# Moving 88 additions of an expert sum from VectorE to GpSimd in a one-core vision tower kernel

## The reference

```
h = _L0_tok_ref(x, ...)                                 # spectral layers, then an MLP
h = _layernorm(h + _L0_attn_ref(h, Wq, bq, Wk, bk, Wv, bv))
h = _layernorm(h + _L0_ffn_ref(h, gate_w, gate_b, w1, b1, w2, b2))   # 8 experts, top 1, with a capacity
h = _layernorm(h + _L1_attn_ref(h, W0, b0, W1, b1))                  # two layers of a gated recurrence
h = _layernorm(h + _L1_ffn_ref(h, ..., gamma, beta))                 # 16 experts, top 2, own norm inside
```

## Time and profile before

| what | value |
|---|---|
| time, median of 3 runs | 2967.37 us (2964.72 to 2968.38) |
| profiled execution, time | 2959.79 us |
| its span in the trace | 2958.0 us |
| PE busy over the span | 2663.2 us (90%) |
| DVE busy | 2114.4 us (71%) |
| ACT busy | 1995.4 us (67%) |
| POOL busy | 69.5 us (2%) |
| token part (2540 us to the end): PE, DVE, POOL busy of 418 us | 360.66, 342.26, 20.76 us |

### The profile page before, as it was taken

How to read it: one execution, slowest core, us unless ns; L and a number is a source line. 1 busy time by engine, 2 the same in 40 slices (tenths; PEclk the granted TensorE clock), 3 DMA queues, 4 the chain that set the end, 5 groups by cost and what they waited for, 6 DMA issues and landing times.

```text
span 2958.0 us, 75928 instructions
## 1 busy us (share of the span) xinstructions
PE 2663.2 (90%) x28642; PEld 1565.3 (53%) x28642; DVE 2114.4 (71%) x4202; ACT 1995.4 (67%) x2415; POOL 69.5 (2%) x93
## 2 busy tenths in 40 slices
PE   5777789999898999898999977999999999899985
PEld 3444456666566666666666654444444444454432
DVE  6999776888776888766888854454544544488887
ACT  5888675677565777655777755787787878555652
POOL 0000000000000000000000002000000000100000
PEclk9999999999999999999999999999999999999997
DMA  3422264754355754455755542411111110012232
GB/s 98 134 104 110 76 206 156 246 182 171 134 189 168 223 186 175 163 165 161 219 194 183 182 152 55 100 61 51 47 50 51 61 51 14 26 35 89 71 93 57
DMA packets 122800, 361.57 MB, mean 122 GB/s; under 512 B 45878, under 2 KB 73814, under 8 KB 86806
## 3 DMA queue, kind: packets, MB, share of 16 engines
q1 hardware_dynamic: 99542, 185.95, 20.1%
q10 hardware_dynamic: 18432, 134.23, 11.2%
q0 software_dynamic: 4672, 39.20, 6.1%
HBM read 204.77 MB, written 154.53 MB: 121 GB/s over the span
## 4 chain that ended last, share of the span: by engine, by line
PE 74%; DVE 11%; issue 7%; ACT 6%; DMA 2%; ACTq 0%; SPq 0%; DVEq 0%; POOL 0%; POOLq 0%
PE pA L1540 16%; PE pA L1548 8%; PE pT L1635 8%; PE pS L1577 7%; PE pD L1624 5%; PE pD L1591 4%; PE pT L1566 4%; PE pD L1511 3%; PE pD L1606 3%; PE pA L1566 2%; DVE arena L1907 2%; PE pT L1645 2%; ACT h_rows L1724 2%; DMA h_scratch<-h_new 1%; PE pS L1465 1%
## 5 line engine op out<-in xcount | busy, mean ns | idle before, releaser
L1874 DVE TENSOR_REDUCE small<-arena 128x32 f32<-128x1056 f32 x320 | 397.1, 1243 | 310.1 <-ACT arena L1709 303.5
L1540 PEld LDWEIGHTS pA<-conv_bd,h_in 128*128 128x128 f32 x4096 | 481.5, 193 | 95.3 <-issue 95.3
L1540 PE MATMUL pA<-conv_bd,h_in 128*128 128x128 f32 x4096 | 518.3, 280 | 2.1 <-DVE arena L1867 1.7
L1699 ACT COPY w_sb<-pA 128x1024 f32<-128x1024 f32 x256 | 259.4, 1013 | 249.9 <-PE pA L1548 232.5
L1720 ACT ACTIVATE h_new<-pT,bet,gam 128x1024 f32<-128x1024 f32 x256 | 307.1, 1200 | 148.9 <-PE pT L1566 132.4
L1888 DVE SCALAR_TENSOR_TENSOR w_sb<-w_sb,small 128x1024 f32<-128x1024 f32 x320 | 386.8, 1209 | 4.5 <-DVE h_new L1896 2.3
L1709 ACT ACTIVATE arena<-w_sb 128x1024 f32<-128x1024 f32 x320 | 338.9, 1059 | 10.2
L1577 PEld LDWEIGHTS pS<-cst,h_new 128*128 128x128 f32 x2048 | 220.4, 141 | 203.1 <-issue 133.3
L1566 PE MATMUL pT<-cst,w_sb 128*128 128x128 f32 x2048 | 276.1, 279 | 39.1 <-DVE w_sb L1888 20.2
L1577 PE MATMUL pS<-cst,h_new 128*128 128x128 f32 x2048 | 280.3, 280 | 23.3 <-ACT h_new L1720 20.8
L1566 PEld LDWEIGHTS pT<-cst,w_sb 128*128 128x128 f32 x2048 | 231.0, 143 | 104.1 <-DVE w_sb L1888 49.1
(11 more groups left out here) (325 smaller groups left out, 3427.9 us busy)
## 6 DMA issues: line engine op xcount, KB each, us to landing
h_scratch<-h_new ACTq DMA_DIRECT2D x128, 1024.0 KB, 4.4
h_in<-h_scratch SPq DMA_DIRECT2D x128, 1024.0 KB, 5.0
w_sb<-gates_scratch SPq DMA_DIRECT2D x168, 128.0 KB, 3.0
y_scratch<-w_sb POOLq DMA_DIRECT2D x32, 576.0 KB, 8.5
y_in<-y_scratch SPq DMA_DIRECT2D x512, 36.0 KB
w_sb<-in_L_tok_w1r_dram POOLq DMA_DIRECT2D x8, 576.0 KB, 7.0
w_sb<-in_L_tok_w1i_dram POOLq DMA_DIRECT2D x8, 576.0 KB, 6.7
w_sb<-in_L_tok_w2r_dram POOLq DMA_DIRECT2D x8, 576.0 KB, 6.9
```

What stands on the lines that cost most here:

```text
L1540: pe.matmul(pA[:, c:c + 128], h_in[:, 1024 * n + c:1024 * n + c + 128], conv_bd[:], start=(j == 0), stop=False, skip_group_check=True)
L1699: act.copy(raw[n], pA[:]).then_inc(s["copied"], 1)
L1874: dve.reduce_sum(var[n], sq[n % 2], axis=AX).then_inc(s["summed"], 1)
```

## The change

DVE no longer makes the additions of the expert sum. It multiplies each expert's bank with the gates into one of four buffers (two more than before, z3c and z3d, placed behind the other parameters), and POOL adds the buffer to Y. ADDS numbers the additions; a new semaphore `added` counts them. DVE waits before a product until the addition that read its buffer four before is done, and before the bias until all additions so far are done. POOL waits for its own previous addition and until DVE has freed the bank of this step. The gate stores stay in POOL's queue, now between additions. TOKEN_ORDER is a new list with the same steps in another order.

```
-        b2a, b2b, ge2 = param(P, S), param(P, S), param(P, 512)
+        b2a, b2b, ge2, z3c, z3d = param(P, S), param(P, S), param(P, 512), param(P, 512), param(P, 512)
...
-        Z3 = [w_sb[:, 2 * CW + CW * i:3 * CW + CW * i] for i in range(2)]
+        Z3 = [w_sb[:, 2 * CW + CW * i:3 * CW + CW * i] for i in range(2)] + [z3c, z3d]
...
+            if key[0] in ("out1", "out2"):
+                ADDS.append(ADDS[-1] + (key[2] > 0) if ADDS else -1)
...
                     if e == 0:
                         dve.tensor_tensor(y, b[:], GB[i % NGB], ALU.mult).then_inc(s["td_free"], 1)
-                        own_freed()
                     else:
-                        dve.tensor_tensor(Z3[e % 2], b[:], GB[i % NGB], ALU.mult).then_inc(s["td_free"], 1)
-                        own_freed()
-                        dve.tensor_tensor(y, y, Z3[e % 2], ALU.add)
+                        if ADDS[i] >= len(Z3):
+                            dve.wait_ge(s["added"], ADDS[i] - len(Z3) + 1)
+                        dve.tensor_tensor(Z3[ADDS[i] % len(Z3)], b[:], GB[i % NGB], ALU.mult).then_inc(s["td_free"], 1)
...
             def add_bias(c):
                 b = take()
-                link(dve.memset(score[:, 0:1], 0.0))
+                dve.wait_ge(s["added"], ADDS[used[0] - 1] + 1)
...
+                elif key[0] in ("out1", "out2"):
+                    i = uses
+                    uses += 1
+                    if key[2] > 0:
+                        if ADDS[i] > 0:
+                            pool.wait_ge(s["added"], ADDS[i])
+                        pool.wait_ge(s["td_free"], n_d + 4)
+                        pool.tensor_tensor(chunk(Y, c), chunk(Y, c), Z3[ADDS[i] % len(Z3)], ALU.add).then_inc(s["added"], 1)
```

Of the list, the last line before and now:

```
-    e2.2 e2.2 e2.3 e2.3 e2.3 eb2.2 e2.3 e2.3 e2.3 e2.3 yb2.2 e2.3 e2.3 e2.3 e2.3 e2.3 e2.3 e2.3 e2.3 e2.3 eb2.3 yb2.3
+    e2.2 eb2.2 e2.3 e2.3 yb2.1 e2.3 e2.3 e2.3 e2.3 e2.3 yb2.2 e2.3 e2.3 e2.3 e2.3 e2.3 e2.3 e2.3 e2.3 e2.3 eb2.3 yb2.3
```

More of the change, by code:

```diff
@@ L179 @@
 TOKEN_ORDER = """
[L180 to L187, removed]
-    e2.2 e2.2 e2.3 e2.3 e2.3 eb2.2 e2.3 e2.3 e2.3 e2.3 yb2.2 e2.3 e2.3 e2.3 e2.3 e2.3 e2.3 e2.3 e2.3 e2.3 eb2.3 yb2.3
+    xt1.0 qkv.0 xt1.1 sc.0 ex.0 qkv.1 pt.0 pv.0 xt1.2 qkv.2 xt1.3 wg.0 xt2.0 sc.1 gq1.0 gl1.0 ex.1 sc.2 pt.1 gx1.0 ex.2 cum.0 pv.1
+    qkv.3 gt1.0 pt.2 e1.0 xt2.1 e1.0 pv.2 gq1.1 e1.0 e1.0 sc.3 ex.3 gl1.1 gx1.1 e1.0 cum.1 pt.3 e1.0 pv.3 xt2.2 e1.0 e1.0 gt1.1
+    eb1.0 e1.1 e1.1 yb1.0 e1.1 e1.1 xt3.0 gq1.2 gru0.0 gl1.2 e1.1 gru1.0 e1.1 gback.0 gx1.2 e1.1 cum.2 xt4.0 xt2.3 gq2.0 gt1.2
+    gl2.0 gq1.3 gx2.0 gm2.0 e1.1 eb1.1 gt2.0 e2.0 e2.0 e2.0 e2.0 e2.0 e2.0 yb1.1 e2.0 e2.0 gl1.3 e2.0 gx1.3 xt3.1 e2.0 e2.0 e2.0
+    gru0.1 e2.0 e2.0 e2.0 e2.0 gru1.1 cum.3 e1.2 e1.2 gback.1 e1.2 e1.2 eb2.0 xt4.1 yb2.0 e1.2 e1.2 gt1.3 e1.2 e1.2 eb1.2 e1.3
+    e1.3 gq2.1 yb1.2 e1.3 gl2.1 e1.3 xt3.2 e1.3 gru0.2 e1.3 gru1.2 gx2.1 e1.3 gm2.1 gback.2 e1.3 eb1.3 gt2.1 e2.1 e2.1 e2.1 e2.1
+    e2.1 e2.1 yb1.3 xt4.2 e2.1 e2.1 xt3.3 e2.1 gru0.3 gq2.2 e2.1 e2.1 gru1.3 gl2.2 e2.1 e2.1 gx2.2 gm2.2 e2.1 e2.1 gback.3 e2.1
+    gt2.2 e2.2 e2.2 e2.2 e2.2 e2.2 e2.2 xt4.3 e2.2 e2.2 gq2.3 e2.2 e2.2 e2.2 gl2.3 gx2.3 gm2.3 e2.2 eb2.1 e2.2 gt2.3 e2.2 e2.2
+    e2.2 eb2.2 e2.3 e2.3 yb2.1 e2.3 e2.3 e2.3 e2.3 e2.3 yb2.2 e2.3 e2.3 e2.3 e2.3 e2.3 e2.3 e2.3 e2.3 e2.3 eb2.3 yb2.3
 """
@@ L424, in build @@
         g2_dram = nc.dram_tensor("gates2_scratch", [NCH, E2, CT * P], F32, kind="Internal").ap()
-        GT_PLACE, EB_FREED, sends_d = {}, {}, 0
+        GT_PLACE, EB_FREED, ADDS, sends_d = {}, {}, [], 0
         for key in token_steps():
@@ L442, in build @@
                   "scored", "gru_act", "gru_out", "ones_set", "passed",
-                  "attended", "fed", "recurred", "pair_subbed", "pair_exped", "pair_gated", "mixed1", "mixed2",
+                  "attended", "fed", "recurred", "pair_subbed", "pair_exped", "pair_gated", "mixed1", "mixed2", "added",
                   "gates_stored", "ge10_loaded", "ge11_loaded", "ge20_loaded", "ge21_loaded"] + [f"g_loaded{i}" for i in range(NGB)]
@@ L1031, in token_pool @@
                 pool.tensor_tensor(lo.bitcast(F32R), w, hi, ALU.subtract).then_inc(s["w1_split"], 1)
-            n_s = 0
+            n_s, n_d, uses = 0, 0, 0
             for key in token_steps():
+                n_d += TOKEN_SENDS.get(key[0], (0, 0))[0]
                 n_s += TOKEN_SENDS.get(key[0], (0, 0))[1]
```

## The result

The changed kernel took 2980.62 us, the median of 10 runs (2969.03 to 2987.24); the kernel before took 2967.84 us beside it, also 10 runs (2953.95 to 2971.68). The ratio is 1.0051 with a 95% interval of [1.0033, 1.0069]: slower by half a per cent.

What follows compares the result with a forecast made beforehand. PE was taken to bound the middle, three DVE normalisations the end. End steps gave 2954.4, less 5 for the middle: 2949.4 of span, 8.6 less than before; off the median, 2958.8 us, 8-in-10 range 2949 to 2973.

Steps and rivals of the forecast that it cites:

- The middle: Token part before 2865 us: fewer PE waits against new DVE and GpSimd waits, 5 us gained; bounds 13 gained, 5 lost.
- Goes: VectorE loses 0.72 us per expert, 63 us in all, mostly where PE bounds, which buys nothing by itself.
- Comes: Each 128x512 addition on GpSimd takes 1.27 us, one following another at 1.36 us.
- The shared path: Products run freely beside GpSimd's additions; two-SBUF instructions of a normalisation wait for them, 1.7 us in the sum.
- rival (d): Products and additions exclude each other, each addition costing 2.0 us instead of 1.36: 2992 us, chance 0.05.
- rival (c): Stores and additions delay each other in GpSimd's queue; bias waits 44 us, locks 18 us: 2975.8 us, chance 0.14.
- The end, steps 2 to 6: From `yb2.1` through `yb2.2` and nine experts to the last bias, then 25.55 us unchanged: span end at 2954.4.
- Step 1: PE finishes sending expert 1 of chunk 3 at 2881.8 instead of 2893.67, as stops and slow clock go.

Runs made afterwards that it cites:

- e1: The changed kernel with gate stores issued by ScalarE behind its copy, GpSimd having only additions: 2956.98 us, ratio 0.998 to the kernel before.
- e5: The kernel before, additions still on VectorE, with only the gate stores moved from GpSimd to ScalarE: 2966.41 us, ratio 1.000 to the kernel before.
- e11: The changed kernel measured and profiled again without an edit: 2975.67 us, ratio 1.0042 to the kernel before.
- e2: The changed kernel with the old list of steps, gate stores still on GpSimd: 2971.2 us, ratio 1.0027 to the kernel before.
- e4: The changed kernel with the old list of steps and gate stores issued by ScalarE: 2962.3 us, ratio 0.9992 to the kernel before.

## Why the prediction was wrong

The step that failed is the one named "The middle": "I take 5 us gained", with a loss of 5 as its bound, "if two new stops of 2.5 us appear". Three appeared, of 2.25, 2.88 and 6.24 us, each with slow matmuls behind it. TensorE's waits in the middle came to 18.2 us, where they were 10.2, and its clock to 0.96 where it was 0.99, another 9 us by the prediction's own measure (0.03 of 290 us). So the 5 us gained were some 13 us lost. `yb2.1` started 354.7 us behind the cast (2895.76 - 2541.05) where the steps put it at 336.9 (2877.6 - 2540.71): 18 us late. Without GpSimd's place and wait (e1) it started at 2881.91 - 2544.84 = 337.1 us. That agreement with the forecast is partly luck: the sum started from one profile with a token part of 417.3 us, and e5, timed the same, had 407.7. Timed, e1 gains 0.2%, about 6 us, where 8.6 were forecast.

The working had the parts. It said that GpSimd stands still at each store and that the loads behind it take 3.0 us. But it priced the store's landing, and never asked what stands *ahead* of the store in GpSimd's queue. The answer was in the new list: `gback.3 e2.1 gt2.2` and `gback.2 e1.3 eb1.3 gt2.1` put one product behind a normalisation on VectorE, its addition ahead of the store on GpSimd. The step also took "TensorE bounds this stage" as cover for VectorE's waits; a wait for gates isn't covered by VectorE's idle time, because TensorE runs out of banks.

Point by point:
- **Goes.** Right: VectorE's busy time over the span fell from 2114.4 to 2065.9 us, by 48.5; 60.9 us of additions went, and 8.3 of the other 12.4 us are in instructions that became longer beside GpSimd's (below). In the middle it bought nothing by itself, as said.
- **Comes.** Right: additions took 1.28 us (1.27 forecast), one behind another at 1.35 (1.36):

```profile
L1051 POOL TENSOR_TENSOR h_new<-h_new,spec 128x512 f32<-128x512 f32 x44 | 56.4, 1283 | 109.5 <-DVE spec L914 105.1 <-DVE w_sb L914 1.4 <-DMA gates_scratch<-h_in 1.3
```

- **The shared path.** Right, and with it rival (d) is out: products beside additions took 0.69 us. The second early instruction of `yb2.2` waited for the addition that had started before it, and ended 0.55 us behind it (2915.62 + 1.62 = 2917.24 against 2916.12 + 1.67 = 2917.79):

```profile
2914.72 1.37 DVE L809 SCALAR_TENSOR_TENSOR h_new<-w_sb,h_new 128x512 f32<-128x512 f32 x1
2916.12 1.67 DVE L810 TENSOR_TENSOR w_sb<-h_new 128x512 f32<-128x512 f32 x1
```

The two lost 0.68 + 0.98 = 1.66 us; 1.7 was forecast. The rule of the Trainium skill, SBUF — State Buffer, "Who interferes with whom", agrees with these rows. The prediction applied it to `yb2.2` and, in rival (c), to some 25 steps for 18 us. Over the token part the VectorE groups that the change left alone grew by 8.3 us (L993, a product of the gates, from a mean of 292 ns to 760). In e1 they grew by 9.6 us, and e1 has not the loss: the shared path was no part of it.
- **The end, steps 2 to 6.** `yb2.1` to the next product 13.6 us (13.8), to the product behind `yb2.2` 19.2 (19.4), to the last bias 13.0 (13.1), to the end 25.55 (25.55). All right. Step 1 can't be judged apart from the middle. The forecast that `yb2.1` starts near 2878 us failed with the middle.
- **Rival (c)** was the nearest, at 0.14 and 2975.8 us. It said that stores and additions share a queue, and took the price from waits at the biases, 44 us, and locks, 18 us. The waits at the biases came to 19.0 us and the locks to 8.3, and most of it cost nothing: e1 has 16.7 and 9.6 us of them. The price came through the expert that needed the gates, and through the one bias that waited behind a landing.

## What to carry to other kernels

Before moving compute onto an engine that issues DMAs, list for each DMA what will now stand ahead of it in that engine's program. Then ask when the work that these instructions wait for gets done on its own engine: a short store behind an addition that waits for a normalisation is as late as the normalisation. Give a latency-critical store to the engine that makes its data, or put it ahead, and put the wait for its landing ahead of the next store and not ahead of the next piece of work. And ask of each added buffer which wait it shortens: where the consumer needs the last result, two did as well as four.

## What was not expected of the hardware

- The profile of one execution is coarse here. Between the two profiles of the changed kernel the execution was 12 us longer in e11 (2980.99 against 2969.03), but the token part was 2.8 us shorter; the first cast came 14.9 us later. The same order of work took 417.3 us in one (before) and 407.7 in another (e5, with the store moved and the timed ratio 1.000), with clock dips at different places.
- From the issue of a gate store by GpSimd to the product that needs it took 6.4 us (2849.91 to 2856.30): 1.84 to the first load's issue, 1.0 until the loads of expert gates begin, 3.5 until the product.
- Where its next addition was ready, GpSimd's wait for the landing of a store cost 1.28 to 2.99 us of its time, beyond 0.55 for the issue.
- Open: why e2 is 0.35% slower than e4, with profiles that differ by 1 us of token part. The landing wait is a candidate, since e2 has it and e4 has not, but with the old list it wasn't tried alone; and products of expert 0 wait 4.5 us for gates in e2, 1.6 in e4. The profile of e2 is of its quickest run, 11 us under its median.
